# Six operand slots instead of four in the second product of a two-layer adapter kernel

## The reference, cut to what matters

```
# x: (32, 128, 2048) float32; id7 in 1..7 and id14 in 1..14 pick adapters for each of the 32 batches
x = x + (x @ W0.T + bias + scale[id7] * (x @ A[id7].T) @ B[id7].T)   # W0 2048x2048, A 16x2048, B 2048x16 for each id
x = x + x @ W1[id14].T                                              # W1: 16 matrices of 2048x2048
```

## Time and profile before

| | |
|---|---|
| runs shown | 2745.59, 2750.38, 2751.7 us |
| median | 2750.38 us |
| profiled execution | 2752.24 us |
| its span, first to last instruction | 2750.4 us |
| mean granted TensorE clock | 0.998 |
| TensorE busy | 2718.7 us (99%) |
| VectorE busy | 1822.5 us (66%) |
| ScalarE busy | 1339.7 us (49%) |
| GpSimd busy | 738.8 us (27%) |
| DMA | 645 MB in the span, 235 GB/s |

### The profile page before, as it was taken

How to read it: one execution, slowest core, us unless ns; L and a number is a source line. 1 busy time by engine, 2 the same in 40 slices (tenths; PEclk the granted TensorE clock), 3 DMA queues, 4 the chain that set the end, 5 groups by cost and what they waited for, 6 DMA issues and landing times.

```text
span 2750.4 us, 34206 instructions
## 1 busy us (share of the span) xinstructions
PE 2718.7 (99%) x12057; PEld 2246.1 (82%) x12057; DVE 1822.5 (66%) x1628; ACT 1339.7 (49%) x1413; POOL 738.8 (27%) x589
## 2 busy tenths in 40 slices
PE   8999999999999999999999999999999999999999
PEld 6788888888888888888888888888888888888887
DVE  6767776866665657686756565768675646666766
ACT  3333355756442336666643232666664323356665
POOL 4345711411612111141251221114134112111321
PEclk9999999999999999999999999999999999999999
DMA  8858956666845435666784543899997554499997
GB/s 297 327 198 294 334 167 216 218 210 225 315 159 194 154 113 190 208 221 212 231 304 156 191 157 131 295 302 315 314 323 271 173 174 163 142 305 313 303 321 246
DMA packets 198108, 645.17 MB, mean 235 GB/s; under 512 B 23185, under 2 KB 33585, under 8 KB 197937
## 3 DMA queue, kind: packets, MB, share of 16 engines
q1 hardware_dynamic: 197936, 642.98, 68.9%
HBM read 651.28 MB, written 58.72 MB: 258 GB/s over the span
## 4 chain that ended last, share of the span: by engine, by line
PE 89%; DVE 4%; DMA 3%; POOL 2%; ACT 1%; issue 1%; SPq 1%; ACTq 0%; POOLq 0%; DVEq 0%
PE acc L855 16%; PE acc L857 16%; PE acc L856 16%; PE acc L801 13%; PE acc L812 13%; PE acc L802 13%; DMA raw<-w 3%; DVE ws L736 2%; PE acc L772 2%; POOL raw L519 1%; POOL raw L502 1%; PE acc L810 1%; DVE ops L736 1%; DMA raw<-xt 1%; ACT ws L607 0%
## 5 line engine op out<-in xcount | busy, mean ns | idle before, releaser
L736 DVE TENSOR_TENSOR ws<-raw,ws 128x1024 fp32r<-128x1024 f32 (+1 forms) x1008 | 1304.6, 1317 | 430.6 <-ACT ws L607 426.9
L607 ACT CAST ws<-raw 128x1024 fp32r<-128x1024 f32 (+1 forms) x1008 | 1027.7, 1044 | 1145.0 <-PE acc L812 516.5
L855 PE MATMUL acc<-ws,ops 128*128 128x512 f32 (+1 forms) x2048 | 798.2, 390 | 6.8 <-DVE ws L736 6.6
L856 PE MATMUL acc<-ws,ops 128*128 128x512 f32 (+1 forms) x2048 | 796.9, 389 | 0.0
L857 PE MATMUL acc<-ws,ops 128*128 128x512 f32 (+1 forms) x2048 | 796.8, 389 | 0.0
L801 PE MATMUL acc<-ops,ws 128*128 128x512 f32 x1792 | 700.8, 391 | 13.2 <-DVE ops L736 6.8
L812 PE MATMUL acc<-ops,ws 128*128 128x512 f32 x1792 | 699.8, 391 | 0.0
L802 PE MATMUL acc<-ops,ws 128*128 128x512 f32 x1792 | 698.8, 390 | 0.0
L519 POOL TENSOR_TENSOR raw<-raw,eye_s 128x128 f32<-128x128 f32 x384 | 358.6, 965 | 1257.3 <-DMA raw<-w 1256.7
L502 POOL TENSOR_TENSOR raw<-raw 128x1024 f32<-128x1024 f32 (+1 forms) x116 | 309.0, 2664 | 561.6 <-DMA raw<-xt 463.8
L855 PEld LDWEIGHTS acc<-ws,ops 128*128 128x128 f32 x2048 | 384.4, 188 | 90.7 <-issue 7.7
(11 more groups left out here) (60 smaller groups left out, 660.3 us busy)
## 6 DMA issues: line engine op xcount, KB each, us to landing
raw<-w SPq DMA_DIRECT2D x928, 512.0 KB
raw<-xt SPq DMA_DIRECT2D x172, 512.0 KB
raw<-w_sums SPq DMA_DIRECT2D x104, 512.0 KB
out<-ost SPq DMA_DIRECT2D x128, 256.0 KB, 5.8
w_sums<-raw SPq DMA_DIRECT2D x32, 512.0 KB, 5.0
x_sums<-raw SPq DMA_DIRECT2D x16, 512.0 KB, 3.9
raw<-x_sums SPq DMA_DIRECT2D x16, 512.0 KB
raw<-a SPq DMA_DIRECT2D x80, 64.0 KB
```

The lines of the kernel that those rows point to most:

```text
L607: ins = eng.copy(hi, src)
L736: ins = eng.tensor_tensor(lo, src, hi, ALU.subtract) if hi is not None else eng.tensor_copy(lo, src)
L855: eng.matmul(acc, yh, wh, start=begin, stop=False)
L856: eng.matmul(acc, yh, wl, start=False, stop=False)
```

## The change

The two LoRA-B buffers `bs` become slots 4 and 5 of `ws`. The second product counts through six slots, the first product (W and LA blocks) through slots 0 to 3 as before; the count starts from 0 whenever the kind changes. Six slots are two units, so `j` = 1 is always in slot 1 or 4 and `j` = 2 in slot 2 or 5, one above it. The second flag, its registers and the instruction that makes it go. The key of an S split may lie up to 13 us ahead of its block instead of 8. The first use of slots 4 and 5 in a group waits for the last LoRA-B matmuls of the group (`k` = 5, and `LB` of `k` = 6); the LoRA-B splits of the next group wait for the last S block of this one.

```diff
+NS = 6
-LEAD = 8.0
+LEAD = {"W": 8.0, "LA": 8.0, "S": 13.0}
...
-    slot_of = {b: n for n, b in enumerate(slots)}
-    def slot_done(n):
-        b = slots[n]
-        return at[b[:5] + (2,)] if b[0] == "S" and b[5] == 1 else at[b]
+    bs_done = ["W", "LB"]
+    slot_of, prior_of, last, count = {}, {}, [None] * NS, 0
+    for n, b in enumerate(slots):
+        if b[0] == "S" and slots[n - 1][0] != "S":
+            last[NWS:] = [at[bs_done[i], b[1], LORA_K[2 + i], HT - 1] for i in range(2)]
+        count = 0 if n and (b[0] == "S") != (slots[n - 1][0] == "S") else count
+        slot_of[b] = count % (NS if b[0] == "S" else NWS)
+        prior_of[b] = last[slot_of[b]]
+        last[slot_of[b]] = at[b[:5] + (2,)] if b[0] == "S" and b[5] == 1 else at[b]
+        count += 1
...
-        free = te[slot_done(n - NWS)] if n >= NWS else -100.0 + n
-        splits.append((max(free + 0.2, ts[at[b]] - LEAD if n > 1 else -100), ts[at[b]], b[0], b[1:]))
+        free = te[prior_of[b]] if prior_of[b] is not None else -100.0 + n
+        splits.append((max(free + 0.2, ts[at[b]] - LEAD[b[0]] if n > 1 else -100), ts[at[b]], b[0], b[1:]))
...
-        ws = sb("ws", [P, NWS, 2, 1024], F32R)
+        ws = sb("ws", [P, NS, 2, 1024], F32R)
-        bs = sb("bs", [P, 2, 2, 1024], F32R)
-        order_i = sb("order_i", [1, 5, NB], I32)
+        order_i = sb("order_i", [1, 4, NB], I32)
+        bs = ws[:, NWS:NS]
...
-                    m = slot_of[(kind,) + index]
-                    if m >= NWS:
-                        eng.wait_ge(s_mm, slot_done(m - NWS) + 1)
+                    m = prior_of[(kind,) + index]
+                    if m is not None:
+                        eng.wait_ge(s_mm, m + 1)
...
                     elif g:
-                        eng.wait_ge(s_mm, at["LB" if i else "W", g - 1, LORA_K[i + 2], HT - 1] + 1)
+                        eng.wait_ge(s_mm, at["S", g - 1, 1, C1 - 1, NU - 1, 2] + 1)
...
-            eng.wait_ge(s_order, 4)
-            eng.tensor_scalar(order_i[:, 4, 0:T], order_i[:, 3, 0:T], -3.0, 3.0, ALU.mult, ALU.add)\
-                .then_inc(s_order, 1)
...
-            eng.wait_ge(s_order, 5)
-            differ, turned = load_flags(eng, 3, 1), load_flags(eng, 4, 3)
+            eng.wait_ge(s_order, 4)
+            differ = load_flags(eng, 3, 1)
...
-                            m = (n - 1) % NWS
-                            q = 2 * (2 * g + h) + 1
-                            slot = differ[q] + m if m < n else turned[q]
+                            slot = differ[2 * (2 * g + h) + 1] + (n - 1)
```

More of the change, by code:

```diff
@@ L520, in _ @@
                         ins.then_inc(s_pool, 1)
+        bs = ws[:, NWS:NS]
         def a_view(n):
-            return ws[:, n % NWS, 0, :].rearrange("p (t n) -> p t n", t=HT)
+            return ws[:, n, 0, :].rearrange("p (t n) -> p t n", t=HT)
         def split_views(n):
@@ L554, in split_views @@
             else:
-                k = slot_of[(kind,) + index] % NWS
+                k = slot_of[(kind,) + index]
                 v, hi, lo = t, ws[:, k, 0, :], ws[:, k, 1, :]
@@ L777, in _ @@
                     _, g, k, o = blk
-                    n, h, acc = slot_of[blk] % NWS, HT * half_of(g, k), bank_of(blk)[:]
+                    n, h, acc = slot_of[blk], HT * half_of(g, k), bank_of(blk)[:]
                     if o == 0 and k not in (2, 5):
@@ L840, in _ @@
                     eng.wait_ge(s_lo, number[blk] + 1)
-                    n = slot_of[blk] % NWS
+                    n = slot_of[blk]
                     for s2 in range(2):
```

## The result

The changed kernel took 2742.76 us, the median of 12 runs (2736.68 to 2747.6), against 2750.69 us for the kernel before in 12 (2745.59 to 2757.05): a ratio of 0.997, 95% interval 0.9961 to 0.9979. That is 7.9 us less. A second set of 12 runs on another occasion gave 2743.4 and 0.9978 (0.9969 to 0.9986). The forecast was 2741.3 in a range of 2736 to 2751. The total came out right: the ring gave back about what was forecast or somewhat more, and the earlier start, put at nothing, took some 3 us away again. The profiled execution shown here took 2746.84 us, near the upper end of the twelve, with a span of 2745.0.

A forecast was written before the change was run, and what follows sets the result against it. TensorE, busy 99%, was taken to bound the kernel, leaving only its waits: of 11.3 us cost, 6.0 + 3.1 = 9.1 regained, so 2750.4 - 9.1 = 2741.3 us, range 2736 to 2751.

The forecast's parts named there:

- the ring: Second product: six slots regain 6.0 us at half boundaries and 3.1 at group ends, 9.1 of 11.3 us of wait cost.
- LoRA-B in slots 4 and 5: Sharing the slots adds waits with nothing due behind them: 0; if wrong, less than 2.4 us a group.
- `j` = 2 addressing: Addressing of the `j` = 2 blocks: one register plus a constant, as before; 0.
- the earlier tile: Half boundary: the first diagonal raw tile lands, and GpSimd's run begins, 2.7 us earlier.
- the cast that passes a `Y` cast and three copies: ScalarE at the half boundary: new keys bring the `j` = 2 cast forward by 2.6 us at most.
- `LEAD` = 13: Planner's keys: acts only on the first five S splits of a group, where no wait stands; 0.
- The shared time: Rival, 20%: VectorE and GpSimd alternation eats the lead at the boundaries; only 4.6 us regained, 2746 us.
- Transfers: Rival, 10%: raw tiles and transfers, not slots, set how far ahead splits reach; 2750 us.
- The slower case: Rival, 8%: VectorE without gaps slows GpSimd's additions in 16 single diagonal runs, 1 us each; 2755 us.
- The second flag: Kernel start: fewer register loads start the first product 3.8 us earlier, costed at nothing; bounds 0 and 3.8.
- the wait list: Sign: TensorE loses most of the eight waits before L855 and the one of 1.72 us before L801.
- the GpSimd run from 506.8: Sign: GpSimd's boundary runs start near 507 us and are still 27 to 29 us long.

The follow-up runs named there:

- late start: Changed kernel with the second flag made and loaded again but unused, first product starting at 19.2 us: 2737.21 us (0.9959), repeated 2742.84 us (0.9966).
- old order: Changed kernel with six slots and their waits, but the planner's keys computed as for four slots with 8 us of lead: 2743.69 us, ratio 0.9974.
- new order without the slots: Kernel before, four slots and their waits, with planner's keys computed as for six slots with 13 us of lead: 2778.68 us, ratio 1.01.
- Starting at 17.9: Changed kernel whose first matmul waits for all eight half tiles of activations instead of four: 2743.51 us, ratio 0.9974.

## Why the prediction was right, and where it was not

*The ring: mechanism right, term of the right size or somewhat small.* The eight waits before L855 and the 1.72 and 0.26 us behind a second product went. I forecast 9.1 of 11.3 us regained. Over the runs it was 11.3 and 9.4 with the late start; the pair of profiles shows 12.9. In that pair two sizes were off. The cost of 11.3 was too low: set beside the changed kernel matmul by matmul, the ten listed waits cost 11.6 us, 0.30 each beyond their idle time instead of 0.27, and the other 1.3 lies in one wait of 0.12 us at 702 and in delays that show no idle time. And the 2.2 us I kept as residue (0.3 at four boundaries, 1.0 at the end of g = 2) are 0 in every one of the ten profiles with six slots: from S is 2375.0 or 2375.1 us in all. The four-slot profiles scatter, 2383.5, 2386.0 and 2388.0, so the ring is worth 8 to 13 us by the execution, and the pair shown is at the upper end. I had worked the boundary against a VectorE that never idles; it does, 1.44 us before its split at 535.2. The terms put at nothing for LoRA-B in slots 4 and 5 and for the `j` = 2 addressing held: TensorE waits at no change of group.

*Two paths credited where one sufficed.* I gave 2.7 us to the earlier tile and 2.6 to the cast that passes a `Y` cast and three copies. With the old order the waits were gone all the same, so the second was not needed. The new order without the slots is harmful. Taking `LEAD` = 13 as without effect agrees with that run too, which had 8.

*The rivals on the ring.* The shared time did not decide: the GpSimd run is as long as before and the lead covers it. Transfers did not stop it: 0.91 and 0.93 busy in g = 2, and no wait. The slower case had its premise wrong. Its additions of 1.4 us were those of the single runs between the boundaries; in the boundary run the median is 1.44 us again, but most single runs of the first groups have medians of 0.46, and the mean over all 384 additions fell from 965 to 931 ns.

*The second flag: the step that failed.* I wrote "What starts earlier waits longer there. Bounds 0 and 3.8", and excluded a loss without a reason. The first half was right: the start moved from 19.16 to 15.26 us, as forecast (15.3), and none of it was kept. But it cost 7.5 us in the profile shown, and about 3 us over the runs: 1.0011 with four slots, 2.9 us (0.6 to 5.3) with six. What the profiles show in its place is a wait of 3.8 us instead of none at the third block, and stretches at 1.2 GHz behind such waits. A later step is visible as well. VectorE's split before `lows` (start, us; the `ops` line) took 1.21 us in the kernel before and 3.44 after, where a GpSimd sum started at 123.74 just before it:

```profile
120.26 1.21 DVE L736 TENSOR_TENSOR ops<-raw,ops 128x1024 fp32r<-128x1024 f32 x1
121.40 2.58 DVE L683 TENSOR_TENSOR lows<-acc,mask 32x256 fp32r<-32x256 f32 x6
```

```profile
123.78 3.44 DVE L739 TENSOR_TENSOR ops<-raw,ops 128x1024 fp32r<-128x1024 f32 x1
127.14 2.58 DVE L686 TENSOR_TENSOR lows<-acc,mask 32x256 fp32r<-32x256 f32 x6
```

```profile
123.74 2.40 POOL L506 TENSOR_TENSOR raw<-raw 128x1024 f32<-128x1024 f32 x1 [2.70 <-DMA raw<-xt]
```

That agrees with the rule of the Trainium skill that the prediction cites ("SBUF — State Buffer", "Who interferes with whom"): the one that starts second is held up for the other's whole instruction, 2.2 of 2.4 us here. With a wait of 3.4 us for `lows` behind it, where there was 1.1, it explains part of the loss at 131 us.

*What the spread is made of.* The two sets with the second flag back are one kernel with one start at 19.2, and yet their profiles reach S at 356.0 and 363.6. Smaller differences ahead of it even out; at 47 us the traces part for good. First the one at 356.0, then the one at 363.6, VectorE's split and GpSimd's sum:

```profile
46.89 1.23 DVE L742 TENSOR_TENSOR ws<-raw,ws 128x1024 fp32r<-128x1024 f32 x1
47.20 3.17 POOL L506 TENSOR_TENSOR raw<-raw 128x1024 f32<-128x1024 f32 x1 [1.84 <-DMA raw<-xt]
```

```profile
46.98 2.39 POOL L506 TENSOR_TENSOR raw<-raw 128x1024 f32<-128x1024 f32 x1 [1.85 <-DMA raw<-xt]
47.16 3.29 DVE L742 TENSOR_TENSOR ws<-raw,ws 128x1024 fp32r<-128x1024 f32 x1
```

Where VectorE is first, its split takes 1.23 us; where GpSimd is first by 0.18 us, it takes 3.29. The transfer issued behind that split leaves at 48.14 or at 50.47, and the next sum starts at 51.39 or at 53.84. At 120 us the same happens to the split before `lows`, 1.21 against 3.42 us. These two turns are 2.3 and 2.2 of the 7.6 us; I did not follow the rest. All eleven profiles with the mask in one block fall in line with them. With VectorE first at 47 and quick at 120 stand 356.0, 358.3 and 359.3; with only the second, 358.9 and 360.6; with neither, the six from 362.5 to 366.3. The start is not what sorts them: 359.3 started at 14.8 and 363.6 at 19.2.

Ten profiles agree on what follows S, and the device time is 2381.0 or 2381.1 us more than the time to S in each of them. If that holds in the executions without a profile, an estimate, the changed kernel's 24 reached S from 355.7 to 366.7, median 362.3. The profile shown, at 365.8, is one of the late ones, which is why its start looks like a loss of 7.5 us and not of 3.

*What stays open.* No run forced the order of the two engines, so that it causes the spread is shown by one pair of equal kernels and a sorting of profiles made afterwards. How an earlier start makes the bad order likelier, if it does, is not shown. Keeping TensorE busy in the wait gave back 3 us, which fits the clock's part, but its profile is also one with both good turns. Starting at 17.9, with no slow stretch at the third block, gave nothing.

*The signs named beforehand.* Right: the wait list, the start at 15.3, the GpSimd run from 506.8 (507 forecast). Wrong: ScalarE still waits 1.66 us on a slot in a sweep, since a longer ring moves that wait and doesn't end it; the run is 29.9 us long, above the 27 to 29 given; and the first group reached the second product at 365.8, not 358. The total of 2741.3 was close in part by luck. Some 3 us for the start were not charged, and the ring gave somewhat more than its 9.1 us, 9.4 to 11.3 over the runs.

## What to carry to other kernels

A ring that is two slots longer removes a wait when the feeding engines fall behind in bursts and catch up between them; count the burst's deficit against the lead in time, and take the lead alone as the mechanism before crediting a new order. The planner's free times must be those of the real ring: an order that runs ahead of its slots blocked in-order queues and cost 28 us. Where a start is made earlier in front of a stretch that is bound elsewhere, bound it below nothing: the wait only moves, and it can be dearer in its new place. And before a difference of a few us between two profiles is put down to the change, profile one of the kernels twice.

## What the runs showed of the hardware that was not expected

- TensorE waited 3.79 us, and the window of 30 to 37 us behind it has a granted clock of 0.52, 1.2 GHz of 2.4; 12 matmuls started there for 33 in the kernel before. With TensorE kept busy in the wait there was no such stretch. The length of a wait does not decide alone: in that same run, of two waits of 2.9 us one had 6.8 us at 1.2 GHz with it and the other none.
- GpSimd's addition of 128x128 has a median of 0.46 us where no VectorE instruction overlaps it and 1.44 in step with VectorE, and a VectorE split of 1.2 us took 3.44 us behind a GpSimd sum of 2.40. Which of the two starts first, by as little as 0.2 us, moved the next transfer by 2.3 us.
- Six-slot kernels with the same second product ran from 2734 to 2748 us. All ten profiles agree to 0.1 us from the second product's start on, so the spread in them comes from the first 366 us.
